# Attention start-up reordered: loads, GpSimd/VectorE/ScalarE order up to the first scores, tokens ahead of cached keys, idle transposes

## The reference

```
q = x Wq (32 heads of 128), k = x Wk, v = x Wv (8 heads of 128)
q = rope(rmsnorm(q) * q_norm_w, pos), k = rope(rmsnorm(k) * k_norm_w, pos)
pos = cache_seqlens[b] + token
keys, values = 512 cached (gathered by a block table) followed by the 128 new ones
scores = q k^T / sqrt(128); cached keys at or past cache_seqlens[b] are masked
x = x + softmax(scores) v Wo
```

## Time and profile before

| | us |
|---|---|
| median of 3 runs | 1445.78 (1444.72 to 1446.23) |
| profiled execution, its time | 1446.6 |
| profiled execution, its span | 1444.8 |
| TensorE busy | 1387.1 |
| VectorE busy | 987.1 |
| ScalarE busy | 852.9 |
| GpSimd busy | 669.4 |

### The profile page before, as it was taken

The page is one execution under the profiler, slowest core; times in us unless marked ns, Lnnn a source line. Parts: engine busy times, 40 slices in busy tenths (PEclk is TensorE's granted clock), DMA queues, the critical chain, the costliest instruction groups (busy, mean ns, idle before and its releaser), DMA issues. The chain is left out here.

```text
span 1444.8 us, 25475 instructions
## 1 busy us (share of the span) xinstructions
PE 1387.1 (96%) x7864; PEld 1206.2 (83%) x7864; DVE 987.1 (68%) x2069; ACT 852.9 (59%) x2200; POOL 669.4 (46%) x963
## 2 busy tenths in 40 slices
PE   4999999999999999999999999999998869999998
PEld 3888888888888888888888888888887657888886
DVE  6777777777777777777777777777775645545544
ACT  6655666666676656666665666666554636434444
POOL 5755465465556555655565555555442550000102
PEclk9999999999999999999999999999999989999999
DMA  5345225423631462155235423631120553543522
GB/s 180 102 154 167 59 78 172 118 73 95 195 102 29 145 191 70 20 169 174 58 86 179 107 64 102 210 81 30 31 58 1 184 176 101 167 145 108 168 90 102
DMA packets 162395, 163.93 MB, mean 113 GB/s; under 512 B 121632, under 2 KB 129440, under 8 KB 152096
## 3 DMA queue, kind: packets, MB, share of 16 engines
q1 hardware_dynamic: 156096, 125.97, 29.7%
q0 software_dynamic: 5952, 35.65, 7.7%
q10 hardware_dynamic: 288, 1.57, 0.3%
HBM read 131.71 MB, written 31.46 MB: 113 GB/s over the span
## 5 line engine op out<-in xcount | busy, mean ns | idle before, releaser
L492 ACT ACTIVATE at_pT_hi<-at_ps 128x512 fp32r<-128x512 f32 x320 | 178.4, 600 | 175.6 <-PE at_ps L887 175.4
L421 POOL TENSOR_SCALAR at_probs<-at_probs,at_row_inv 128x640 f32<-128x640 f32 x256 | 205.9, 804 | 155.5 <-DVE at_row_inv L717 147.3
L711 DVE CUSTOM_DVE_ANT_0 at_scores<-at_ps,at_mask,at_inv_rms 128x640 f32<-128x640 f32 x256 | 224.0, 878 | 67.7 <-PE at_ps L65 65.9
L661 DVE TENSOR_TENSOR at_pT_lo<-at_ps,at_pT_hi 128x512 fp32r<-128x512 f32 x320 | 208.1, 683 | 90.8 <-ACT at_pT_hi L492 90.8
L535 ACT ACTIVATE at_probs<-at_scores,at_neg_max 128x640 f32<-128x640 f32 x256 | 213.2, 833 | 57.4 <-DVE at_neg_max L711 55.8
L63 PE MATMUL at_ps<-at_kT_hi,at_qT_hi 128*128 128x320 f32 x512 | 164.6, 322 | 0.4 <-DVE at_kT_lo L661 0.2
L887 PE MATMUL at_ps<-ident,at_probs 128*128 128x128 f32 x1280 | 160.5, 272 | 2.0 <-POOL at_probs L421 2.0
L65 PE MATMUL at_ps<-at_kT_hi,at_qT_lo 128*128 128x320 f32 x512 | 158.2, 309 | 0.0
L64 PE MATMUL at_ps<-at_kT_lo,at_qT_hi 128*128 128x320 f32 x512 | 158.1, 309 | 0.0
L887 PEld LDWEIGHTS at_ps<-ident,at_probs 128*128 128x128 f32 x1280 | 145.2, 141 | 11.1 <-POOL at_probs L421 2.7
L63 PE MATMUL at_ps<-at_pT_hi,at_v_hi 128*128 128x512 f32 x320 | 131.8, 412 | 1.8 <-DVE at_pT_lo L661 1.8
(11 more groups left out here) (212 smaller groups left out, 3490.3 us busy)
## 6 DMA issues: line engine op xcount, KB each, us to landing
kT_pages<-at_kv_stage SPq DMA_DIRECT2D x14, 1024.0 KB
v_pages<-at_kv_stage SPq DMA_DIRECT2D x14, 1024.0 KB
at_k_raw<-kT_pages SPq DMA_DIRECT2D x56, 256.0 KB, 3.1
at_v_raw<-v_pages SPq DMA_DIRECT2D x56, 256.0 KB, 3.9
sw_wgu_raw<-in_sw_gu SPq DMA_DIRECT2D x22, 512.0 KB, 3.4
staging<-in_L_cond_Wo SPq DMA_DIRECT2D x8, 1024.0 KB, 5.6
ds_mask_raw<-in_mask_Bx4096x_ik SPq DMA_DIRECT2D x8, 1024.0 KB, 5.4
staging<-in_L_cond_Wq SPq DMA_DIRECT2D x7, 1024.0 KB, 6.8
```

What stands on the lines that cost most here:

```text
L421: pool.tensor_scalar(probs[:, h, :], probs[:, h, :], row_inv[:, h:h + 1], 1.0, ALU.mult, ALU.mult).then_inc(probs_done, 1)
L492: act.activation(out, src, ACT.Copy).then_inc(done, 1)
L661: dve.tensor_tensor(out, src, hi_part.bitcast(F32), ALU.subtract).then_inc(done, 1)
L711: dve.tensor_tensor_reduce(out=scores[h % 2][:], in0=slot(h), in1=mask[:, b, :], scale=inv_rms[b % 2][:, h:h + 1], scalar=3.0e38, op0=ALU. ...
```

## The change

SyncE issues all first loads: constants, tokens 0, Wq, Wkv, tokens 1 to 7, with no wait in between. The multiplications of the norm weights move to GpSimd, in front of `key_idx`; GpSimd issues the two gathers of sequence 0, then `page_row`, then splits Wkv, and issues the gathers of sequence 1 after that. VectorE makes the angles in one piece before tokens 0 and Wq; in its later order `turn_q` goes in front of tokens 1, and `table(1)` behind `new_kv`. ScalarE splits tokens 0 before the masks, makes six masks instead of five there, splits Wkv in front of Wq, loads the table of the exponential later, and splits the cached values of sequence 0 after the first exponentials. The semaphore of the high parts of Wq and Wkv becomes two. In every sequence of group 0 that has them, tokens come before cached keys on ScalarE and VectorE. TensorE transposes the identity 40 times into the bank of y before its first real work. Context is cut; semaphore declarations are left out.

```diff
             load_tokens(0)
-            sp.wait_ge(wqkv_loaded, 32)
+            load_qkv(0)
             for b in range(1, B):
...
                 cs = slice(2 * (n - DC), 2 * (n - DC) + 2)
-                wait_apart(pool, wqkv_hi_done, g * QKV_GROUPS + n + 1, pool_passed)
+                wait_apart(pool, wkv_hi_done, g * KV_GROUPS + n - DC + 1, pool_passed)
                 pool.tensor_tensor(wkvT_lo[:, cs, :], wkv_raw[:, cs, :], wkvT_hi[:, cs, :].bitcast(F32), ALU.subtract).then_inc(wkv_done, 1)
...
             pool.wait_ge(small_loaded, 32)
+            pool.tensor_scalar(kqw_sb[:, 0:D], kqw_sb[:, 0:D], float(np.sqrt(D)), 1.0, ALU.mult, ALU.mult).then_inc(norms_ready, 1)
+            pool.tensor_scalar(kqw_sb[:, D:2 * D], kqw_sb[:, D:2 * D], -1.0, 1.0, ALU.mult, ALU.mult).then_inc(norms_ready, 1)
             pool.tensor_scalar(key_idx[:], table_sb, float(HK * PSIZE // LC), block_f, ALU.mult, ALU.add).then_inc(idx_ready, 1)
+            pool.wait_ge(idx_ready, 1)
+            gather(0, k_rows, k_raw, k_loaded)
+            gather(0, v_rows, v_raw, v_loaded)
             pool.tensor_scalar(page_row[:], page_col, float(2 * HK), 1.0, ALU.mult, ALU.add).then_inc(page_step, 1)
-            pool.wait_ge(idx_ready, 1)
-            pool.wait_ge(page_step, 1)
-            for b in range(2):
-                gather(b, k_rows, k_raw, k_loaded)
-                gather(b, v_rows, v_raw, v_loaded)
             for n in range(KV_GROUPS):
                 qkv_group(0, DC + n)
+            gather(1, k_rows, k_raw, k_loaded)
+            gather(1, v_rows, v_raw, v_loaded)
+            pool.wait_ge(page_step, 1)
             rotate_q(0, 0)
...
                     act.wait_ge(q_in_psum if n < DC else kv_in_psum, g * B)
-                hi(out, src, wqkv_loaded, g * 32 + 32, wqkv_hi_done)
+                hi(out, src, wqkv_loaded, g * 32 + 32, wq_hi_done if n < DC else wkv_hi_done)
...
-            act.dma_start(wq_raw[:], wq[bass.ds(0, 1)].rearrange("o p c d -> p (o c) d")).then_inc(wqkv_loaded, 16)
-            act.dma_start(wkv_raw[:], wkv[bass.ds(0, 1)].rearrange("o p c d -> p (o c) d")).then_inc(wqkv_loaded, 16)
             act.wait_ge(iota_done, 4)
...
             act.wait_ge(mask_bias_done, 1)
-            masks(range(5))
             tokens(0)
-            for n in range(QKV_GROUPS):
+            masks(range(6))
+            for n in (DC, DC + 1, 0, 1, 2, 3):
                 qkv_group(0, n, first=True)
...
                 act.activation(out[:, :, 1, HALF:D], t.rearrange("p (b f) -> p b f", b=B), ACT.Sin).then_inc(sincos_ready, 1)
-            act.activation(warm[:, 1], minus_half[:], ACT.Exp)
             tokens(1)
             cached_keys(0, 0)
-            masks(range(5, B))
             new_kv(0, 0)
             squares(0, 0)
+            masks(range(6, 7))
             queries(0, 0)
+            masks(range(7, B))
             new_keys(0, 0)
+            act.activation(warm[:, 1], minus_half[:], ACT.Exp)
             squares(0, 1)
-            cached_values(0, 0)
...
                         exps(g, b, h)
+                    if by_row(g) and b == 0:
+                        cached_values(0, 0)
                     if more:
                         queries(g1, b1)
-                        cached_keys(g1, b1)
                     if by_row(g) and b < B - 2:
                         tokens(b + 2)
+                    if more:
+                        cached_keys(g1, b1)
                     weights(0)
...
                                        invf_sb.unsqueeze(1).broadcast_to([P, B, HALF]), ALU.mult))
-                dve.tensor_scalar(kqw_sb[:, 0:D], kqw_sb[:, 0:D], float(np.sqrt(D)), None, ALU.mult)
                 link(dve.tensor_scalar(turns, angle, 1.0 / TWO_PI, ROUND, ALU.mult, ALU.add))
-                dve.tensor_scalar(kqw_sb[:, D:2 * D], kqw_sb[:, D:2 * D], -1.0, None, ALU.mult)
                 link(dve.tensor_scalar(turns, turns, -ROUND, None, ALU.add))
-                for part in (PI_A, PI_B):
+                for part in (PI_A, PI_B, PI_C):
                     link(dve.scalar_tensor_tensor(out=angle, in0=turns, scalar=-part, in1=angle, op0=ALU.mult, op1=ALU.add))
-
-            def bound_angles():
-
-                link(dve.scalar_tensor_tensor(out=angle, in0=turns, scalar=-PI_C, in1=angle, op0=ALU.mult, op1=ALU.add))
                 dve.tensor_scalar(sin_t, angle, PI_F32, -PI_F32, ALU.min, ALU.max).then_inc(angles_ready, 1)
...
+                dve.wait_ge(norms_ready, 2)
                 dve.wait_ge(sincos_ready, 2)
...
             def qkv_group(g, n):
-                cs = slice(2 * (n - DC), 2 * (n - DC) + 2)
-                out, src, h = (t[:, n, :] if n < DC else t[:, cs, :] for t in ((wqT_lo, wq_raw, wqT_hi) if n < DC else (wkvT_lo, wkv_raw, wkvT_hi)))
-                lo(out, src, h, wqkv_hi_done, g * QKV_GROUPS + n + 1, wq_done if n < DC else wkv_done)
+                out, src, h = (t[:, n, :] for t in (wqT_lo, wq_raw, wqT_hi))
+                lo(out, src, h, wq_hi_done, g * DC + n + 1, wq_done)
...
             tokens(0)
-            qkv_group(0, 0)
-            qkv_group(0, 1)
-            bound_angles()
-            qkv_group(0, 2)
-            qkv_group(0, 3)
+            for n in range(DC):
+                qkv_group(0, n)
             table(0)
-            tokens(1)
             turn_q(0, 0, 0)
             turn_q(0, 0, 1)
+            tokens(1)
             cached_keys(0, 0)
+            new_kv(0, 0)
             table(1)
-            new_kv(0, 0)
             queries(0, 0)
...
                         queries(g1, b1)
-                        cached_keys(g1, b1)
                     if first and b < B - 2:
...
                         table(b + 2)
+                    if more:
+                        cached_keys(g1, b1)
                     weights(0)
...
+            for n in range(10):
+                for h in range(G):
+                    pe.transpose(bank(Y_BANK)[:, h * S:(h + 1) * S], ident[:], ident[:])
             cached_keys(0, 0)
```

More of the change, by code:

```diff
@@ L177, in attention @@
         mask_bias_done = sem("mask_bias_done")
+        norms_ready = sem("norms_ready")
         mask_done = sem("mask_done")
@@ L182, in attention @@
         wo_loaded = sem("wo_loaded")
-        wqkv_hi_done = sem("wqkv_hi_done")
+        wq_hi_done = sem("wq_hi_done")
+        wkv_hi_done = sem("wkv_hi_done")
         wq_done = sem("wq_done")
@@ L235, in attention @@
         KV_GROUPS, WO_GROUPS = DC // 2, G
-        QKV_GROUPS = DC + KV_GROUPS
         def xT_raw(b):
```

## The result

| | before | after |
|---|---|---|
| median of 5 runs, us | 1445.78 (1444.11 to 1446.57) | 1452.99 (1451.78 to 1453.46) |
| profiled execution, its time | 1446.6 | 1451.78 |
| its span | 1444.8 | 1450.0 |

The ratio is 1.005 (95% interval 1.0035 to 1.0064): slower by 7.2 us, where 8.6 us less were forecast.

A forecast was written before the change was run, and what follows sets the result against it. TensorE, busy 96% of the span, was taken as the bound, so only its idle or slow places could pay. 5.1 + 3.5 = 8.6 us off the profiled 1446.6 gave 1438.0, as median 1437.2; range 1434.7 to 1440.9.

The forecast's parts named there:

- It cost nothing to run them, since nothing else wants TensorE then: Claim that the 40 identity transposes before TensorE's first real work add no time.
- they buy nothing: Claim that 3.3 us of idle after the transposes drops TensorE's clock again, leaving the first projection cold.
- a slow queue: Rival, 3%: the single load queue delivers Wq and Wkv late; at 110 GB/s the time is 1449.1 us.
- a stretch from 160 us on that is longer than before: Listed sign of error: TensorE's work after the start should have kept its length.
- the sum: Start 5.1 plus tokens ahead of cached keys 3.5: 8.6 us off the whole kernel, giving 1437.2 us.
- The start: Up to the first scores: earlier loads and first projection save 5.1 us.
- The chain behind it: From the queries' turn to the first mask-and-maximum: costs 0.25 us, between 0.0 and 0.7.
- The cached values behind the exponentials: Sequence 0, ScalarE: splitting cached values later costs 0, at worst 0.5 us.
- Tokens ahead of keys: Sequences 1 to 5 of group 0: five TensorE idle times of 0.71 us vanish, saving 3.5 us.
- The clock: Rival, 18%: TensorE's clock stays up for the first projection, 1.5 us more gained, 1435.7 us.
- VectorE and GpSimd did not block each other: Rival, 16%, said they would block each other at the start, delaying the projection: 1.2 us less gain, 1438.4 us.

The follow-up runs named there:

- b_before_idle: Kernel before the change with only the 40 identity transposes added in front of TensorE's first work: 1458.94 us, ratio 1.01.
- a_no_idle: Changed kernel without its 40 transposes of the identity: 1438.13 us, ratio 0.9953.
- i_values_back: Changed kernel with the transposes in a hardware loop and sequence 0's cached values split ahead of the first exponentials again: 1436.39 us, ratio 0.9943.
- k_both: Changed kernel, transposes looped 72 turns of one, cached values ahead of exponentials again, token loads 2 to 7 held until gathered keys land: 1454.74 us.
- h_idle_loop: Changed kernel with its identity transposes in a hardware loop of 18 turns of four: 1437.77 us, ratio 0.9947.
- j_hold_tokens: Changed kernel with transposes looped (18 turns of four) and token loads of sequences 2 to 7 held until the gathered keys land: 1436.1 us.
- n_incs196: Changed kernel with 196 increments of an unused semaphore on TensorE's queue in place of the transposes: 1491.19 us.
- e_incs20: Changed kernel with 20 increments of an unused semaphore on TensorE's queue in place of the transposes: 1440.58 us.

## Why the prediction was wrong

**The step that failed** is "It cost nothing to run them, since nothing else wants TensorE then". I priced the 40 transposes by their time, which is idle, and not by their place in TensorE's program. That they buy nothing was right (4.25 us of idle, then a projection at the lower level of the clock). That they cost nothing was wrong: code in front of the loop made TensorE fetch the loop's instructions anew in five passes, for 14.4 us (`b_before_idle`, 1458.94 against 1444.53 of the kernel before beside it) to 14.9 (changed kernel, 1452.99, against `a_no_idle`, 1438.13). The kernel before showed a sign: q8's 31 packets on the page, none for five passes. I had a rival on the slower side, a slow queue, but it was the wrong mechanism; the queue moved its load in time (constants used at 4.03, forecast 3.8). One of my signs of being wrong did come: a stretch from 160 us on that is longer than before.

**Without that step** the sum held: at the end of the first pass 8.1 us were won, forecast 8.6, and `a_no_idle` has 1438.13, forecast 1437.2. That it came so near is partly luck: its two terms were off by 2.0 and 1.5 us in opposite directions.

*The start* gave 3.1, not 5.1, at the first scores of sequence 1 (45.67 to 42.59). The keys were ready at 12.67, not 11.3: the gather was issued at 5.96 (forecast 5.6) and took 6.7 us. My own rows gave 5.6 + 6.1 = 11.7, and I took 11.3 without a reason that the rows carry; likewise the constants at 3.8, where 2.5 + 0.4 + 0.5 is 3.4. So the turn came at 17.79 instead of 16.65: 1.1 us. The chain behind it cost 0.3 (7.74 from turn to first mask-and-maximum, 7.42 before), forecast 0.25. The cached values behind the exponentials cost 0.85 by `i_values_back`, forecast 0, at worst 0.5; the change had won 0.4 elsewhere in sequence 0.

*Tokens ahead of keys* gave 5.0, not 3.5. I added up idle times of 0.71. But the profile's idle time begins at the modelled end of the last matmul in front; from the start of that matmul to the start of the next it was 1.0, and that went.

**The rivals.** The clock stayed down behind 4.25 us of idle and up behind 1.32: both as read from the earlier trace rows. The 16 transposes at 1189.15 already spoke for transposes that raise the clock, and the looped ones show it: they brought it up and, 1.32 us later, it was still up. Their pace matters, as `k_both` shows. The Trainium skill ("TensorE: Matmul & The Clock Gate", Part 4: PE-mode transpose) says that the full clock doesn't engage for transposes, as they don't count as busy in the same way. The rows of `h_idle_loop` are against it.

VectorE and GpSimd did not block each other at L645 and L647 (0.46 and 0.43): L647 ended at 9.75, half a microsecond before GpSimd began its subtractions at 10.26. They did meet at the next place, which I had not priced: the four low parts of Wq took 3.71 us instead of 2.66 (one of them 1.76 instead of 0.68), beside GpSimd's two subtractions, themselves 2.95 instead of 2.49. The cold projection hid it in the changed kernel; in `j_hold_tokens` it sets the pace.

## What to carry to other kernels

An instruction in front of a long hardware loop has a price beside its time: it moves the loop in the engine's program, and a pass that just stays resident may then be fetched anew each time. Before adding code to an engine that is the bound, look at the packets of the instruction queue within the loop's stretch, and after it for waits on "issue" at the pass's head; put filler into a small loop, or behind the large one. To price an idle time on TensorE, take the distance of starts and not the idle time.

## What the runs showed of the hardware

- Five stops at the head of the pass (in `n_incs196` a second in each pass), 1.7 to 3.4 us of idle each, and nine packets of 16.4 KB a pass (ten in one), for a loop of 1725 TensorE instructions; a shift of 256 instructions is none.
- The branch of such a pass lasts 0.2 us when nothing is fetched and 3.4 to 5.0 when the target is.
- Behind a stop of 2.4 us, and 1.5 us behind one of 2.0, TensorE's clock was down for 3.4 us (granted 0.51 and 0.50); behind the three of 1.8 to 2.0 us that followed it stayed up, and so it did behind the one of 3.3 in `e_incs20`.
- A turn of a hardware loop on TensorE with one transpose takes 0.40 us; an increment of a semaphore on its queue 0.15.
- 40 transposes 128x128 in f32 took 6.9 to 7.4 us from idle; 72 in a loop 9.8 to 10.4. Their starts went from 0.21 to 0.11 apart on the way. 72 that were 0.40 apart left the clock at its lower level.
